# Windowed attention and mixture of experts on one core: a new order of the opening, of the keys, of the sum transposes and of the projection

## The chip, the core and the metric

The kernel runs on one core of a Trainium2 chip. The metric is the time of one execution on the device, in microseconds (us). TensorE (PE) does matmuls and transposes and writes to eight PSUM banks; ScalarE (ACT), VectorE (DVE) and GpSimd (POOL) do the rest, GpSimd without access to PSUM; SyncE (SP) issues most of the DMA transfers. Each engine works through its own instructions in order, and the engines are tied to each other by semaphores alone.

## The reference

Two stages, each added to its input. The first is a windowed attention with a mixed score; the second a mixture of eight experts of which two are taken.

```python
t = _ln_c(x) @ W_prep + b_prep            # 5 x 8 heads x 32: q_n, q, k, k_m, v; windows of 8 x 8 tokens
bias, pat_n, pat_m = _spatial(intrinsic)  # relative tables, gathered by the offset of two tokens
score = bias + einsum('bhod,ohid->bohi', q_n, pat_n) \
      + einsum('bhod,bhid->bohi', q, k) + einsum('bhid,ohid->bohi', k_m, pat_m)
score = (score - mean) / sqrt(var(score, ddof=1) + 1e-5)
x = x + (einsum('bohi,bhid->bohd', score, v)) @ W_fin + b_fin
xt = _ln_t(x)                             # 2048 tokens, 64 channels
top 2 of softmax(xt @ Wr + br) -> weights
x = x + sum over the two of weight * (gelu((layernorm(xt) * ln_g + ln_b) @ W1 + b1) @ W2 + b2)
```

## The kernel before

There are 2048 tokens in 32 windows, handled as 16 pairs (`NPAIR`) in four groups (`NG`) of four pairs.

**PSUM.** `make_plan` lists every use of a bank in the order in which TensorE fills it, as (use, bank, readers); from it `begin` takes how often the bank must have been drained, `filled` and `drained` what its readers and their successors wait for. `pe_steps(t)` gives TensorE's uses in step t of the main loop.

**Opening.** x is loaded in four parts, two by SP's queue and two by ScalarE's. VectorE takes the moments of all 16 pairs (`bn_stats`, `bn_aggr`) and then the inverse roots RS by three rounds of an iteration on all 16 columns (`inverse_root`). The normalised XN of pairs 0 to 7 is made by VectorE, of 8 to 11 by ScalarE, of 12 to 15 by GpSimd. GpSimd first makes the identity IDN, issues six small loads (RB, LNB) and then makes the constants CEN, BPS and SEL. TensorE warms up with eight matmuls (`warm`), folds the weights (`weights`, bank 6; ScalarE copies them to WT_ with two copies), and then makes both tables: `table("tm")` and `table("tn")`. The transposes `xt` turn XN into XF.

**Patterns and the round trip.** `pattern("m", m)` makes two tiles of k_m against its table (TAM), for m from 0 to 7. ScalarE copies the even and VectorE the odd tiles to TMG (`copy_moved`), and SP stores each to DRAM (`moved`, L331). When all sixteen stores have landed (`moved_out`), SP loads the same data in another order to SCN (L336), and `pattern("n", m)` may begin: its tiles TNT lie where TMG lay. Behind the n patterns TensorE has the mixed keys (`mixed_keys`, banks 4 to 7, copied to Y), the centred x (`centred`, copied to XC), the shift of the expert bias (`shift_bias`), then the first values and scores. `products` makes the operand AT of the keys behind m pattern 3. Then each n tile is transposed (`turned`), and VectorE adds it to SCN (L1093); every fourth tile (2, 6, 10, 14) goes through a copy HOP by ScalarE to GpSimd (L418). The adds wait for all loads (`moved_in`), the first SR for all adds.

**Main loop, steps 0 to 15.** Step t gives the score of pair t: scores and values (in twos, in even steps), VectorE's SR (L1146), ScalarE's square SQ and copies BV and OR, TensorE's weighted values `o`. For every group j: squares summed on TensorE (`ss`, step 4j+5), copied by ScalarE to SSB, transposed (`st`, L741), from which VectorE makes the variance VB; GpSimd takes the root RSC by a power (L437); VectorE scales to ON (step 4j+9); TensorE turns ON (`on`), ScalarE copies it to ONT, TensorE projects (`y`, L761), VectorE adds to XR (L1182) and takes moments; then normalisation (Z, Z2), transposes (`x2`), the router's logits (`lg`) and its chain on VectorE, tanh on ScalarE, the gates PG (L1175), which GpSimd widens to PW.

**From step 16 on** TensorE has four hidden products of two matmuls each per step (L702, L703), the products down (L714), the gate transposes `gb` (L786), and what is left of the chain above for the later groups.

In steps 6, 10 and 14 of the kernel before, the first of TensorE's uses is this:

```python
        if t % 4 == 2 and t >= 6:
            s.append((("st", (t - 6) // 4), 5, 1))
```

## Time and profile before

| | us |
|---|---|
| median of 3 runs | 210.13 (207.98 to 211.75) |
| profiled execution, its own time | 211.79 |
| its span, first to last instruction | 210.0 |
| TensorE busy | 179.1 (85%) |
| ScalarE busy | 114.5 (55%) |
| VectorE busy | 107.9 (51%) |
| GpSimd busy | 70.5 (34%) |

Busy shares are means over stretches that differ. The order of time shows each engine's work with the idle time ahead of it and what ended that; the chain of waits follows the last instruction back to what released it. A granted clock of 1.00 is 2.4 GHz on TensorE, 0.50 is 1.2 GHz. Matmuls overlap, so that a mean duration is longer than the distance from one to the next.

### The profile page before, as it was taken

The page shows a single profiled execution, that of the slowest core. Times are in us where ns is not written, and L with a number is a line of the kernel's source. Part 1 is how long each engine was busy: PE and PEld are TensorE (multiplying, and loading weights), DVE is VectorE, ACT ScalarE, POOL GpSimd, SP SyncE. Part 2 cuts the span into 40 slices and gives each one's busy share as a digit, 9 for nine tenths or more (in the row PEclk, how much of TensorE's full clock was granted, in tenths as well). Part 3 has the DMA queues.
Part 4 walks back from the last instruction along what each step waited for, and adds up shares of the span by engine and source line. Part 5 has one row for each costly group of instructions (what it writes and reads, how often), then busy time and mean ns, then how long its engine had stood idle before and what let it go on. Part 6 is the DMA issues. An engine that isn't in the chain of part 4 may idle for free.

```text
span 210.0 us, 4283 instructions
## 1 busy us (share of the span) xinstructions
PE 179.1 (85%) x1590; PEld 113.5 (54%) x1590; DVE 107.9 (51%) x298; ACT 114.5 (55%) x225; POOL 70.5 (34%) x104
## 2 busy tenths in 40 slices
PE   6678980899999696758878959999999999999983
PEld 6486430232499574635746925657466745666531
DVE  3642550256637732333476683157864874574333
ACT  2082770246524559573964755765676475666740
POOL 7568100000004700280945928083650056012000
PEclk9856996589999969995896997999999999999999
DMA  6840597699900000200030000000000000000000
GB/s 166 208 116 0 197 331 276 145 227 224 205 4 2 3 0 3 78 25 3 0 101 3 0 5 0 2 0 3 0 25 0 3 0 25 0 2 3 27 0 25
DMA packets 10356, 12.80 MB, mean 61 GB/s; under 512 B 2072, under 2 KB 7712, under 8 KB 10336
## 3 DMA queue, kind: packets, MB, share of 16 engines
q1 hardware_dynamic: 9712, 12.25, 22.0%
q10 hardware_dynamic: 432, 0.27, 0.5%
q8 instruction: 13, 0.21, 0.4%
q14 instruction: 7, 0.06, 0.1%
q0 software_dynamic: 192, 0.01, 0.1%
HBM read 7.81 MB, written 4.72 MB: 60 GB/s over the span
## 4 chain that ended last, share of the span: by engine, by line
PE 65%; ACT 10%; DVE 6%; POOL 6%; issue 6%; SPq 2%; DMA 2%; DVEq 0%; ACTq 0%; POOLq 0%
PE PS L714 12%; PE PS L553 7%; PE PS L702 6%; PE PS L703 6%; PE PS L615 4%; PE PS L786 4%; PE PS L568 4%; PE PS L578 3%; POOL RSC L437 3%; PE PS L761 3%; SPq L331 2%; ACT BV L912 2%; DMA moved<-TMG 2%; PE PS L585 2%; PE PS L642 2%
## 5 line engine op out<-in xcount | busy, mean ns | idle before, releaser
L935 ACT ACTIVATE HR<-PS,B1P 128x512 f32<-128x512 f32 x64 | 39.0, 693 | 5.0 <-PE PS L703 5.0
L714 PE MATMUL PS<-HR,W2s 128*64 128x512 f32 x128 | 31.0, 605 | 0.0
L702 PE MATMUL PS<-X,W1H 128*128 128x512 f32 x64 | 27.4, 428 | 0.0
L703 PE MATMUL PS<-X,W1L 128*128 128x512 f32 x64 | 26.1, 407 | 0.0
L1005 ACT ACTIVATE GB<-PS 128x512 f32<-128x512 f32 x16 | 9.6, 598 | 23.4 <-PE PS L786 23.4
L437 POOL TENSOR_TENSOR RSC<-VB,NHALF 128x32 f32<-128x32 f32 x4 | 21.8, 5461 | 0.3
L425 POOL COPY PW<-PG 128x512 f32<-128x512 f32 x16 | 10.4, 683 | 32.7 <-DVE PG L1175 32.5
L418 POOL TENSOR_TENSOR SCN<-HOP,SCN 128x512 f32<-128x512 f32 x4 | 6.2, 1553 | 44.5 <-ACT HOP L923 44.5
L1146 DVE TENSOR_TENSOR SR<-PS,SCN 128x512 f32<-128x512 f32 x16 | 10.6, 687 | 17.8 <-PE PS L615 14.5
L912 ACT ACTIVATE BV<-PS 64x256 f32<-64x256 f32 x32 | 12.2, 383 | 13.6 <-PE PS L599 13.0
L862 ACT ACTIVATE TMG<-PS 128x512 f32<-128x512 f32 x16 | 10.1, 648 | 16.0 <-PE PS L553 16.0
L553 PE MATMUL PS<-TAN,XF 64*32 64x512 f32 x128 | 10.9, 816 | 6.9 <-DMA moved<-TMG 6.9
L714 PEld LDWEIGHTS PS<-HR,W2s 128*64 128x64 f32 x128 | 7.8, 136 | 13.6 <-issue 12.7
L702 PEld LDWEIGHTS PS<-X,W1H 128*128 128x128 f32 x64 | 12.5, 195 | 3.1 <-issue 0.8
L681 PE MATMUL PS<-BV,SR 128*64 128x66 f32 x256 | 11.7, 242 | 2.6 <-issue 2.2
L786 PEld LDWEIGHTS PS<-IDN,PW 128*128 128x128 f32 x64 | 6.7, 140 | 13.2 <-issue 12.4
L1128 DVE SCALAR_TENSOR_TENSOR GM<-PS,B,GB 128x512 f32<-128x512 f32 x12 | 9.0, 751 | 9.3 <-ACT GB L1005 7.9
L703 PEld LDWEIGHTS PS<-X,W1L 128*128 128x128 f32 x64 | 12.6, 196 | 2.2
L681 PEld LDWEIGHTS PS<-BV,SR 128*64 128x64 f32 x256 | 9.8, 150 | 5.5 <-issue 5.4
L966 ACT ACTIVATE SQ<-SR 128x512 f32<-128x512 f32 x16 | 10.0, 628 | 3.8 <-DVE SR L1146 3.7
L840 DVE COPY TMG<-PS 128x512 f32<-128x512 f32 x8 | 5.6, 698 | 12.2 <-PE PS L553 12.2
L615 PE MATMUL PS<-Y,XF 64*64 64x256 f32 x128 | 11.2, 478 | 0.4 <-DVE SR L1146 0.4
(144 smaller groups left out, 314.6 us busy)
## 6 DMA issues: line engine op xcount, KB each, us to landing
moved<-TMG SPq DMA_DIRECT2D x16, 256.0 KB, 2.8
SCN<-moved SPq DMA_DIRECT2D x16, 256.0 KB, 7.8
W1R<-in_W SPq DMA_DIRECT2D x4, 256.0 KB, 4.0
W1E<-in_W SPq DMA_DIRECT2D x2, 256.0 KB, 5.4
W2s<-in_W SPq DMA_DIRECT2D x1, 512.0 KB, 3.7
out<-XR SPq DMA_DIRECT2D x4, 128.0 KB, 1.8
REL<-in_rel SPq DMA_DIRECT2D x2, 225.0 KB, 5.2
XR<-in_x SPq DMA_DIRECT2D x2, 128.0 KB, 2.4
```

The lines of the kernel that those rows point to most:

```text
L425: G.tensor_copy(PW[:, ep, :, :, :], PG[j % 2][:, :, 2 * ep:2 * ep + 2].unsqueeze(3) .to_broadcast([P, 4, 2, C])).then_inc(gates_wide, 1)
L437: G.tensor_tensor(RSC[:, :, :, :].rearrange("p q h g -> p (q h g)"), vb, NHALF[:, :], ALU.pow).then_inc(rsc_ready, 1)
L553: last = nc.tensor.matmul(PS[before[(kind, 2 * m + r)][0]][32 * u:32 * u + 32, :], XF[rows, :, token], window, start=True, stop=True)
L615: m = nc.tensor.matmul(dst, XF[rows, 2 * (t + a) + b, :], Y[rows, 4 * g:4 * g + 4, t // 2, C * b:C * b + C], start=True, stop=True)
L681: m = nc.tensor.matmul(dst, SR[t % 3][:, (2 * h + b) * C:(2 * h + b) * C + C], BV[t % 4][:, b, h, :, :].rearrange("p g d -> p (g d)"), sta ...
L702: nc.tensor.matmul(ps[:, :], W1H[:, col:col + P], X2[:, j * 512:j * 512 + 512], start=True, stop=False)
L703: end(nc.tensor.matmul(ps[:, :], W1L[:, col:col + P], X2[:, j * 512:j * 512 + 512], start=False, stop=True), "h", n)
L714: m = nc.tensor.matmul(ps[d * C:d * C + C, :], W2s[:, 2 * (2 * ep + d) + c, :], HR[(4 * u + 2 * c + d) % 8][:, :], start=(c == 0), stop=(c ...
L786: m = nc.tensor.transpose(ps[:, q * P:q * P + P], PW[:, a % 4, q, :, :].rearrange("p d c -> p (d c)"), IDN[:, :])
L912: last = A(BV[tv % 4][g * C:g * C + C, :, :, g, 0:HD].rearrange("p b h d -> p (b h) d"), PS[b][g * C:g * C + C, 0:256].rearrange("p (n d) ...
L935: A(HR[n % 8][:, :], PS[b][:, :], ACT.Gelu, bias=B1P[:, col:col + 1]).then_inc(bank_drained[b], 1)
L1146: V_.tensor_tensor(SR[t % 3][:, :].rearrange("p (h b o) -> p h b o", h=4, b=2), PS[t % 2][:, :].rearrange("p (h b o) -> p h b o", h=4, b=2 ...
```

## The change

**Opening.** `inverse_root` is gone. VectorE aggregates each part of x right after its statistics. GpSimd takes the roots by a power with NHALF, first for pairs 0 to 11, then for 12 to 15, and makes RS and NB. VectorE makes XN of pairs 0 to 7, 14 and 15, ScalarE of 8 to 13. The six loads of RB and LNB are issued by ScalarE. `warm` takes a count: 8, then 7 between the bias matmul of `weights` and its other matmuls, and 3 behind it. ScalarE copies the m part of the folded weights first (`wt_ready`), the rest behind its XF copies. Only `table("tm")` stands ahead of the transposes `xt`, which run in the order 0, 2, 1, 3 on banks 4, 7, 5, 0; the copies of tables and XF are divided anew. `table("tn")` stands behind m pattern 1, `products` behind m pattern 4 (their copies behind tiles 2 and 8 on ScalarE).

**Keys.** Mixed keys, centred x and the bias shift stand ahead of the n patterns on TensorE, and their copies ahead of the stores of turned tiles on ScalarE and VectorE. TensorE's own wait for `moved_out` ahead of n is gone; the copies of n keep theirs.

**Adds.** GpSimd's four tiles are 1, 4, 7 and 10 (`HOPS`).

**Steps.** `st` stands at the end of steps 6, 10 and 14, behind `on` and ahead of `x2`; `x2` of group 0 moves from bank 5 to bank 4. On VectorE the addition of the projection and its moments stand ahead of the gates.

```diff
-    plan += [(("tn", h), (4, 5, 7, 6)[h], 1) for h in range(4)]
-    plan += [(("xt", j), j, 1) for j in range(NG)]
+    plan += [(("xt", j), (4, 5, 7, 0)[j], 1) for j in (0, 2, 1, 3)]
...
-        if t % 4 == 2 and t >= 6:
-            s.append((("st", (t - 6) // 4), 5, 1))
...
-        return s + late(10, (("on", 0), 4), (("on", 1), 7)) + late(14, (("x2",), 5)) \
-            + late(11, (("y",), 4)) + late(15, (("lg",), 5))
+        return s + late(10, (("on", 0), 4), (("on", 1), 7)) + late(6, (("st",), 5)) \
+            + late(14, (("x2",), 4)) + late(11, (("y",), 4)) + late(15, (("lg",), 5))
...
+            step(pool.memset(NHALF[:, :], -0.5))
...
-            pool.wait_ge(rx_ready, 1)
-            for q in range(12, NPAIR):
-                last = G.tensor_scalar(XN[:, q, :, :], twice(XR[:, q, :]), RS[:, q:q + 1], NB[:, q:q + 1],
-                                       ALU.mult, ALU.add)
-            last.then_inc(xn3_ready, 1)
+            for part, cols in enumerate((slice(0, 12), slice(12, NPAIR))):
+                pool.wait_ge(mvx_ready, part + 1)
+                step(G.tensor_scalar(VE[:, cols], MV[:, cols, 1], 0.0, EPS_C, ALU.max, ALU.add))
+                step(G.tensor_scalar(RA[:, cols], MV[:, cols, 0], -1.0, None, ALU.mult))
+                G.tensor_tensor(RS[:, cols], VE[:, cols], NHALF[:, cols], ALU.pow).then_inc(rs_ready, 1)
+                pool.wait_ge(rs_ready, part + 1)
+                G.tensor_tensor(NB[:, cols], RA[:, cols], RS[:, cols], ALU.mult).then_inc(rx_ready, 1)
...
             for m in range(8):
                 pattern("m", m)
-                if m == 3:
+                if m == 1:
+                    pe.wait_ge(*drained("wt"))
+                    pe.wait_ge(reln_in, 16)
+                    pe.wait_ge(rel0_in, 16 * 4)
+                    pe.wait_ge(sel_ready, 1)
+                    table("tn")
+                if m == 4:
                     products()
             for h in range(4):
                 pe.wait_ge(*drained("a", h))
             for h in range(4):
                 pe.wait_ge(*drained("tn", h))
-            pe.wait_ge(moved_out, 16 * 16)
-            for m in range(8):
-                pattern("n", m)
             for m in range(8):
                 mixed_keys(m)
             for j in range(NG):
...
             shift_bias()
+            for m in range(8):
+                pattern("n", m)
...
-            for d in range(2):
-                last = A(WT_[:, :, :, d, :], PS[6][:, :].rearrange("p (k g c) -> p k g c", k=4, g=2), ACT.Copy)
-            last.then_inc(bank_drained[6], 1)
...
+            weight_copies(KM, KM + 1).then_inc(wt_ready, 1)
+            for part, qs in enumerate(((8, 9, 10, 11), (12, 13))):
+                act.wait_ge(rx_ready, part + 1)
+                for q in qs:
+                    last = A(XN[:, q, :, :], twice(XR[:, q, :]), ACT.Identity, scale=RS[:, q:q + 1], bias=NB[:, q:q + 1])
                 last.then_inc(xn2_ready, 1)
...
             for j in range(NG):
                 dve.wait_ge(x_in[j], 16)
                 for q in range(4 * j, 4 * j + 4):
                     last = V_.bn_stats(BNX[:, q, :], XR[:, q, :])
-            step(last)
-            for q in range(NPAIR):
-                last = V_.bn_aggr(MV[:, q, :], BNX[:, q, :])
...
-            inverse_root(RS[:, :], VE[:, :], RA[:, :])
...
+                step(last)
                 for q in range(4 * j, 4 * j + 4):
+                    last = V_.bn_aggr(MV[:, q, :], BNX[:, q, :])
+                if j >= 2:
+                    last.then_inc(mvx_ready, 1)
+            for part, qs in enumerate(((0, 1, 2, 3), (4, 5, 6, 7), (14, 15))):
+                dve.wait_ge(rs_ready, 1 if part < 2 else 2)
...
+            dve.wait_ge(moved_out, 16 * 16)
+            for tile in range(1, 16, 2):
+                store_turn(dve, V_.tensor_copy, tile)
             dve.wait_ge(moved_in, N_MOVED)
             for tile in range(16):
-                if tile % 4 == 2:
+                if tile in HOPS:
```

In VectorE's steps the block of `t - 16` (PG) moves, unchanged, from ahead of the block of `t - 12` (XR and `moments`) to behind it. The loop on GpSimd over four hops takes `tile = HOPS[k]`, with `HOPS = (1, 4, 7, 10)`.

## Rows read from the trace of the kernel before

**Rows 1.** The chain of waits: start us, us, what; stores and turned tiles.

```profile
33.40 3.81 DMA moved<-TMG
...
63.65 7.26 PE PS L578 x64
```

**Rows 2.** The order of time, opening: start us, us, engine, line, operation, count, [idle before].

```profile
1.24 0.93 ACTq L857 DMA_DIRECT2D XR<-in_x  x2
...
1.59 3.78 PE L509 MATMUL PS<-IDN 128*128 128x128 f32 x16 [1.59 <-POOL IDN L364]
...
1.77 2.37 POOL L367 DMA_DIRECT2D RB<-in_rel  x4 [0.23 <-issue]
...
4.76 0.60 DVE L1047 BATCH_NORM_STATS2 BNX<-XR 128x6 f32<-128x64 f32 x4 [0.28 <-DMA XR<-in_x]
...
7.89 2.41 PE L502 MATMUL PS<-CEN,WS 64*128 64x64 f32 x16
...
10.34 1.08 ACT L866 ACTIVATE WT__81<-PS 128x512 f32<-128x512 f32 x2 [6.64 <-PE PS L502]
...
11.31 1.64 ACT L871 ACTIVATE XN<-XR,NB,RS 128x128 f32<-128x128 f32 x4
...
16.38 3.49 PE L642 MATMUL PS<-IDN,XN 128*128 128x128 f32 x16
...
20.87 4.31 PE L553 MATMUL PS<-TAM,XF 64*32 64x512 f32 x64 [0.99 <-ACT XF L879]
```

**Rows 3.** Busy time by stretch: us, engines (instructions), granted clock, DMA share, GB/s.

```profile
9.30:19.50 10.20, 8.93 (x69) 8.22 (x68) 4.48 (x18) 5.07 (x11) 6.60 (x14) 0.50 0.25 65
...
37.50:43.40 5.90, 5.85 (x56) 2.13 (x64) 1.70 (x3) 1.55 (x3) 0.00 (x0) 0.50 0.81 184
...
125.20:208.00 82.80, 79.83 (x411) 47.25 (x408) 46.58 (x126) 49.69 (x87) 26.14 (x39) 0.98 0.02 6
```

**Rows 4.** The order of time: stores, loads, and the n patterns.

```profile
22.75 11.10 SPq L331 DMA_DIRECT2D moved<-TMG  x16
...
37.22 11.38 SPq L336 DMA_DIRECT2D SCN<-moved  x16
...
37.55 10.95 PE L553 MATMUL PS<-TAN,XF 64*32 64x512 f32 x128 [6.90 <-DMA moved<-TMG]
```

**Rows 5.** The line of the loads: issues, and time to landing.

```profile
L336 SPq DMA_DIRECT2D SCN<-moved x16: 616/617/1057, 37.2 to 47.5; - x16
...
DMA to landing us min/median/max: 3.8/7.8/11.8
```

**Rows 6.** The order of time: the adds of turned tiles, and the first SR.

```profile
64.34 7.31 DVE L1093 TENSOR_TENSOR SCN<-PS,SCN 128x512 f32<-128x512 f32 x12 [1.94 <-PE PS L578]
...
72.94 1.29 DVE L1146 TENSOR_TENSOR SR<-PS,SCN 128x512 f32<-128x512 f32 x2 [1.28 <-POOL SCN L418]
```

**Rows 7.** TensorE's groups to 125 us: line, form, count | busy, mean ns | idle before.

```profile
L691 PE MATMUL PS<-SQ,ONES 128*32 128x512 f32 x32 | 4.3, 604 | 2.4 <-DVE XR L1182 2.4
L761 PE MATMUL PS<-WF,ONT 128*128 128x64 f32 x32 | 4.0, 277 | 0.7 <-ACT ONT L952 0.7
...
L741 PE MATMUL PS<-IDN,SSB 128*128 128x128 f32 x12 | 2.4, 335 | 7.2 <-ACT SSB L979 7.2
```

**Rows 8.** GpSimd's groups, whole span: the powers of 32 and 4 columns.

```profile
L437 POOL TENSOR_TENSOR RSC<-VB,NHALF 128x32 f32<-128x32 f32 x4 | 21.8, 5461 | 0.3
...
L453 POOL TENSOR_TENSOR RZ<-RZ,NHALF 128x4 f32<-128x4 f32 x4 | 4.2, 1042 | 0.3
```

**Rows 9.** ScalarE's groups from 72 to 125 us.

```profile
L912 ACT ACTIVATE BV<-PS 64x256 f32<-64x256 f32 x27 | 10.3, 383 | 10.2 <-PE PS L599 9.7 <-PE PS L681 0.2
...
L988 ACT ACTIVATE W1H<-W1R,LNG 128x256 fp32r<-128x256 f32 x8 | 3.6, 514 | 0.0
```

**Rows 10.** The order of time: a power on GpSimd beside VectorE's products.

```profile
108.96 1.04 POOL L453 TENSOR_TENSOR RZ<-RZ,NHALF 128x4 f32<-128x4 f32 x1
109.05 1.42 DVE L1166 TENSOR_TENSOR ON<-OR,RSC 128x256 f32<-128x256 f32 x4
```

More of the change, by code:

```diff
@@ L504, in weights, with warm @@
                 end(m, "wt")
-            def warm():
-                for _ in range(8):
+            def warm(times):
+                for _ in range(times):
                     nc.tensor.matmul(PS[7][:, 0:P], IDN[:, :], IDN[:, :], start=True, stop=True)
@@ L644, in _ @@
                 end(m, "xt", j)
+            for h in range(4):
+                pe.wait_ge(*drained("tm", h))
             for j in range(NG):
@@ L664, in _ @@
             shift_bias()
+            for m in range(8):
+                pattern("n", m)
             pe.wait_ge(wv_in, 32)
@@ L893, in _ @@
             A(WRR[:, 0, :], WRs[:, :], ACT.Copy).then_inc(wrh_ready, 1)
-            act.wait_ge(moved_out, 16 * 16)
-            for tile in range(0, 16, 2):
-                store_turn(act, act_copy, tile)
             for m in range(8):
@@ L901, in _ @@
                 A(XC[:, 512 * j:512 * j + 512], PS[j][:, :], ACT.Copy).then_inc(bank_drained[j], 1)
+            act.wait_ge(moved_out, 16 * 16)
+            for tile in range(0, 16, 2):
+                store_turn(act, act_copy, tile)
             def value_copies(tv):
@@ L1020, in _ @@
             V_ = nc.vector
-            def inverse_root(y, v, work):
-                step(V_.tensor_scalar(y.bitcast(I32), v.bitcast(I32), -0.5, float(0x5F3759DF), ALU.mult, ALU.add))
-                for _ in range(3):
-                    step(V_.scalar_tensor_tensor(out=work, in0=y, scalar=-0.5, in1=y, op0=ALU.mult, op1=ALU.mult))
-                    step(V_.tensor_tensor(work, work, v, ALU.mult))
-                    step(V_.scalar_tensor_tensor(out=y, in0=work, scalar=1.5, in1=y, op0=ALU.add, op1=ALU.mult))
             def moments(xin, j):
```

110 lines of the change are left out of this document (52 added, 58 removed).

## The prediction

> **What bounds the kernel now.** I read the chain of waits first, then the order of time engine by engine, then the busy table of chosen stretches, then the groups by line. Four stretches stand out.
>
> The opening ends at 20.87 us, when the first m pattern starts [rows 2]. Ahead of it come, one behind the other, the folded weights, both tables and sixteen transposes, nearly all at a granted clock of 0.50, the lower level of 1.2 GHz [rows 2, 3].
>
> Then comes a round trip through DRAM. The m patterns go out as sixteen stores from 22.75 us on; the last has landed at 33.40 + 3.81 = 37.2 us [rows 1, 4], and only then may TensorE start the n patterns, because TNT is TMG: it sits idle for 6.90 us [rows 4] and comes back at clock 0.50, so that the first n patterns run at half rate [rows 3]. The loads of the same data back are issued from 37.22 us on; the last was issued at 47.5 us and took the longest to land, 11.8 us, so all are in at 59.3 us [rows 5]. VectorE starts to add the turned n tiles to them at 64.34 us [rows 6]. So the loads are 5.0 us early there, and TensorE's queue sets the time: n, keys, centring, bias shift, first values and scores.
>
> Third, steps 0 to 16 of the main loop, from the first SR at 72.94 us [rows 6] to about 125 us. TensorE waits 7.2 us in all for the copies SSB ahead of the sum transposes, which stand at the head of steps 6, 10 and 14, and 2.4 us for XR ahead of the last squares [rows 7].
>
> Last, from 125.2 us on, TensorE is busy for 79.83 of 82.80 us at clock 0.98 [rows 3]: bound by its own work, which the change leaves as it is. An earlier start there passes straight to the end.
>
> **The opening.** GpSimd loses six DMA issues, of which four took 2.37 us [rows 2]. They go to ScalarE's queue, where two issues take 0.93 us: six are 2.8 us, from 2.2 to 5.0 us, then the table load and the dummy Gelu. ScalarE's next work, the weight copy, starts at 10.34 us today [rows 2]; that cover hides them, without it they would cost their 2.8 us. With CEN and BPS some 3.4 us earlier, the bias matmuls follow the eight warm-ups, which end at 5.4 us [rows 2], and seven more warm-ups fill the time until the weights come; I leave the weight matmuls' start at 7.9 us, as today. They took 2.41 us [rows 2], the last of them at the lower clock [rows 3]. With TensorE busy ahead of them I take 1.8 us, end 9.7; the bound above is 10.3.
>
> The roots: sixteen columns of moments are gathered with VectorE's statistics, the third group of which runs at 4.76 us [rows 2]; its own aggregation follows now, so that GpSimd has twelve columns at about 6.1 us. It needs two small operations (0.6 us) and a power. No row shows 12 columns; 32 take 5461 ns and 4 take 1042 ns [rows 8]: the bounds are 5.5 and 1.0 us, and a straight line between them gives 2.3, which I take, since both rows are this operation. The roots are there at 9.1 us; today ScalarE's XN starts at 11.31 [rows 2]. The other four columns follow at 11.2 us.
>
> From there ScalarE is the longest: the weight copy for KM alone (a quarter of the columns of a pair that took 1.08 us [rows 2]; 0.6 us by estimate) to 10.3, six XN at 1.64 / 4 = 0.41 us [rows 2] to 12.8, then two tables and two XF at 0.54, half of that pair, to 14.9. VectorE (ten XN, two tables, two XF) ends about then too. TensorE needs the m table and the transposes ahead of m. Both tables lie between 11.4 and 16.38 us today, the m table being a third of their instructions: 1.7 us, and the transposes take 3.49 us [rows 2]; at the upper clock half of each, 2.6 us, hides under the copies. At the lower clock m starts at 17.1. I take 15.1 us for the first m pattern, a gain of 5.8; the bounds are 14.7 and 17.1.
>
> **The round trip and the fill.** Today the stores are done 16.3 us after the first m pattern (20.87 to 37.2). The n table now sits behind the second m pair (two thirds of 5.0 us, at the upper clock 1.6), while its TAN copies, for which TensorE pauses today, run beside the third and fourth pair: these nearly cancel. The other weight copies (0.9 us on ScalarE) fall before its first m tile is complete. I take 16.0: stores done at 31.1 us. SyncE's queue is otherwise unchanged, so the loads take their 59.3 - 37.2 = 22.1 us again and are in at 53.2 us.
>
> TensorE's m stage takes 37.55 - 6.90 - 20.87 = 9.8 us today [rows 2, 4]; with the n table 11.3, so it is free at 26.4 us. Keys to first scores take 63.65 - 48.50 = 15.1 us (first turned tile less the end of the n patterns [rows 1, 4]), and most of it now stands where the idle time is. The eight n pairs took 10.95 us [rows 4]; without the idle ahead they run like the m patterns, 64 instructions or four pairs in 4.31 us [rows 2]: 8.7. The first turned tile is there at 26.4 + 15.1 + 8.7 + 0.5 = 50.7 us, so now the loads are the later ones, by 2.5 us: VectorE starts at 53.2 instead of 64.34 us. 5.0 of this is the fill, 6.1 the earlier stores. Keys queued ahead of n delay n only where it would have waited; behind ScalarE's and VectorE's waits for the stores no key copy is queued any more. The bias shift takes its wait for LNB along, whose loads now start before 5 us.
>
> **The adds.** Twelve take 7.31 us, and the first SR waits a further 1.28 us for GpSimd's last add [rows 6]. With GpSimd's four at tiles 1, 4, 7 and 10 its last ends before VectorE's. Gain 1.2 us; bounds 0, because VectorE's last four tiles now follow each other, and 1.3. The first SR stands at 60.6 instead of 72.94 us: 12.3 us.
>
> **Sum transposes at a step's end.** I laid out steps 5 to 16, each instruction after its predecessor on its engine and after what it waits for. The scores of step 6 no longer stand behind the first SSB: they start 2.0 us earlier, the first root 1.8. In step 10 TensorE no longer waits for an SSB that itself stands behind the ON products: the second root starts 4.8 us earlier. New waits appear. The projection of step 11 waits for ONT behind ScalarE's value copies (383 ns each), squares and W1H [rows 9]: 3.1 us, where 0.7 is seen today [rows 7]. In step 14 x2, on bank 4 now, waits for ONT's first half, and y waits for X2's low half (0.9 us). The third root comes 5.0 us early, the second group of hidden matmuls 4.8. So of 9.6 us of waits about half is given back. I take 4.5; bounds 0 (all of it returns at ONT) and 7.
>
> What queues behind the later wait for the transposed sums on VectorE is the odd SR; the layout has it 0.2 us late at step 6. Projection ahead of gates: XR and its moments go ahead of PG, which waits for tanh at that point anyway; gb, for which PG is needed, comes two groups of matmuls later, so I cost it at nothing. Uncovered it would cost 1.4 us three times.
>
> **Sum.** 5.0 (fill) + 6.1 (opening) + 1.2 (adds) + 4.5 (steps) = 16.8 us. The profiled execution took 211.79 us, its span 210.0; less 16.8 that is 195.0. The median of the runs is 1.66 below it: 193.3, say 193.5.
>
> **A row against a rule.** While GpSimd's power ran for 1.04 us from 108.96 us on, VectorE's four ON products, two SBUF inputs each, took 1.42 us from 109.05 us on [rows 10]: neither waited for the other. The Trainium skill, "SBUF — State Buffer", section "Who interferes with whom", says that a VectorE instruction with two SBUF inputs and a GpSimd instruction that reads SBUF exclude each other for a whole instruction. The trace does not agree; by the rule rival 3 would hold.
>
> **The rivals.**
> 1. The steps give all back: ONT and the roots become the waits. For it: 2.4 us more at step 11 already; against it: the second root no longer waits behind the scores. 193.5 + 4.5 = 198.
> 2. The clock stays at 0.50 through tables, transposes and the first m pairs. For it: so it was from 9.3 to 19.5 us with TensorE busy for 8.93 of 10.2 us [rows 3]; against it: the added warm-ups. First m at 17.1 and up to 2 us more until the stores are done: 195.5 to 197.5.
> 3. GpSimd's second root chain (1.04 us and three small operations) holds up XN on VectorE, then its tables and XF: +1.6, 195. [rows 10] speak against it.
> 4. The loads flow faster and TensorE sets the adds at 50.7 us: 191.
> 5. Slower than before: the clock stays at 0.50 from the first m pattern to the first turned tile. At the upper clock that stretch is 36 us long; at the lower I estimate 26 us more, since copies hide some. The first SR comes at 86.5 us, 13.5 later than today, less 4.5: 219. It decides from 16.8 us of loss on. The longest such stretch here is 10.2 us, and idle time preceded it [rows 3].
> 6. The opening gives nothing (the power at its upper bound, the weights late): 193.5 + 6.1 = 199.5.
>
> **How the numbers follow.** Forecast 0.50, with a range of its own of 191.5 to 195.5; rivals 1 to 6: 0.18, 0.15, 0.04, 0.07, 0.02, 0.04. The range reaches from below rival 4 to above rival 6, 189.5 to 200.5, with both bounds of the steps in it. A difference of 2%, 4.2 us, is about what a measurement here can tell from no change. Only rival 5 is slower; two rivals at once come near 204. Faster 0.95, same 0.03, slower 0.02.
>
> **What would show it.** Right: first m pattern near 15 us; no TensorE gap at the stores; VectorE's first add waiting for a load; SR not waiting for GpSimd; no idle time ahead of the sum transposes, and ONT the new wait. Wrong: clock 0.50 between 12 and 22 us; a first add at 56 us or later; the second group of hidden matmuls less than 3 us nearer to the first SR.

## The result and the profile after

Four runs of the changed kernel have a median of 201.06 us (200.42 to 201.88), four of the kernel before 210.54 us (207.98 to 211.75). The ratio is 0.959 with a 95% interval of 0.949 to 0.969: faster, by about half of what was forecast (193.5 us), and 0.56 us above the end of the range. The profiled execution took 201.88 us, its span is 200.1 us. The same kernel ran four more times in a later group, on another chip: 198.78 us (197.73 to 200.50), ratio 0.949 (0.939 to 0.959). Single executions that lie more than 1.5% above the fastest of their kernel are left out of ratios, and where fewer than three are left of a kernel below, or of the kernel before beside it, the median stands without a ratio.

The spans are best compared mark by mark. "Again" is the profile of that later group, same code; "held" is the profile of run d2 below, the changed kernel with three edits of mine.

| us | before | forecast | after | again | held |
|---|---|---|---|---|---|
| first m pattern | 20.87 | 15.1 | 15.85 | 15.54 | 14.83 |
| first m pattern to last store landed | 16.33 | 16.0 | 19.13 | 17.26 | 16.83 |
| last store to last load landed | 22.17 | 22.1 | 22.30 | 22.10 | 21.81 |
| last load to VectorE's first add | 4.97 | 0 | 0.03 | 0.02 | 0.02 |
| first add to first SR | 8.60 | 7.4 | 10.72 | 9.61 | 7.94 |
| first SR to second hidden group | 52.23 | 47.7 | 48.29 | 48.34 | 47.70 |
| second hidden group to the end | 84.9 | 84.9 | 83.8 | 83.8 | 83.7 |
| span | 210.0 | 193.2 | 200.1 | 196.7 | 192.8 |

Each row is the difference of two starts or landings in the trace; the forecast is the prediction's own sum, laid out on the same marks. After against forecast, the 6.9 us lost are 0.75 + 3.13 + 0.2 in the opening and the round trip, 3.3 in the adds and 0.6 in the steps, less 1.1 us won in the last stretch.

The order of time of the changed kernel, to be laid beside [rows 2], [rows 4] and [rows 6] (start us, us, engine, line, operation, count, [idle before]):

```profile
5.13 0.60 DVE L1050 BATCH_NORM_STATS2 BNX<-XR 128x6 f32<-128x64 f32 x4 [1.09 <-DMA XR<-in_x]
...
7.83 2.30 POOL L385 TENSOR_TENSOR RS<-VE,NHALF 128x12 f32<-128x12 f32 x1
...
8.01 2.00 PE L499 MATMUL PS<-CEN,WS 64*128 64x64 f32 x16
...
10.17 2.84 DVE L1059 SCALAR_TENSOR_TENSOR XN<-XR,MV,RS 128x128 f32<-128x128 f32 x10 [2.21 <-POOL RS L385]
...
11.29 1.04 POOL L385 TENSOR_TENSOR RS<-VE,NHALF 128x4 f32<-128x4 f32 x1
...
15.85 3.77 PE L550 MATMUL PS<-TAM,XF 64*32 64x512 f32 x32 [1.12 <-ACT XF L889]
...
21.37 1.95 ACT L868 ACTIVATE TAN<-PS 128x450 f32<-128x450 f32 x4 [1.16 <-PE PS L523]
...
42.51 8.79 PE L550 MATMUL PS<-TAN,XF 64*32 64x512 f32 x128
...
52.88 1.97 PE L575 MATMUL PS<-IDN,TMG 128*128 128x128 f32 x16
...
57.31 1.89 DVE L1093 TENSOR_TENSOR SCN<-PS,SCN 128x512 f32<-128x512 f32 x3 [5.18 <-DMA SCN<-moved]
...
58.15 8.21 PE L575 MATMUL PS<-IDN,TMG 128*128 128x128 f32 x48 [3.30 <-DVE SCN L1093]
...
62.69 0.69 DVE L1093 TENSOR_TENSOR SCN<-PS,SCN 128x512 f32<-128x512 f32 x1 [1.01 <-PE PS L575]
...
68.03 1.29 DVE L1148 TENSOR_TENSOR SR<-PS,SCN 128x512 f32<-128x512 f32 x2 [0.30 <-DVE SCN L1093]
...
104.23 0.63 PE L780 MATMUL PS<-IDN,Z 128*128 128x128 f32 x4 [3.55 <-ACT ONT L963]
...
106.36 3.64 PE L762 MATMUL PS<-WF,ONT 128*128 128x64 f32 x16 [0.43 <-DVE X L1206]
...
116.32 0.50 PE L703 MATMUL PS<-X,W1H 128*128 128x512 f32 x1
```

What to see. The reorder of the keys does what the prediction said: the n patterns at 42.51 us follow the keys without idle time and take 8.79 us (8.7 forecast), and VectorE now waits 5.18 us for a load. But TensorE may not run on: four turned tiles fill its four banks, and behind them it stands idle for 3.30 us until VectorE's first add frees one. The next twelve tiles (48 instructions) take 8.21 us, and it is now VectorE that waits for TensorE between its adds (`62.69`, 1.01 us). In step 14 there is a second new wait, x2 for ONT, 3.55 us, and behind it the projection takes 3.64 us for 16 matmuls; the second hidden group starts at 116.32 us.

The busy table shows why both are slow. Columns: stretch, its length, PE, PEld, DVE, ACT and POOL busy (instructions), granted clock, DMA share, GB/s.

```profile
15.80:19.60 3.80, 3.75 (x36) 1.44 (x36) 0.69 (x1) 1.12 (x2) 3.30 (x10) 0.55 0.08 27
...
42.50:51.30 8.80, 8.66 (x134) 3.23 (x135) 5.22 (x9) 4.46 (x7) 0.00 (x0) 1.00 1.14 226
...
58.10:66.40 8.30, 8.25 (x52) 8.12 (x56) 5.61 (x9) 1.79 (x3) 5.30 (x4) 0.65 0.01 2
104.80:115.10 10.30, 9.87 (x61) 8.72 (x60) 6.02 (x19) 4.42 (x9) 4.72 (x1) 0.50 0.01 2
116.30:199.90 83.60, 78.36 (x412) 46.38 (x408) 47.78 (x127) 49.49 (x87) 26.69 (x40) 1.00 0.02 7
```

The n patterns ran at 1.00 (0.50 in the first part of the stretch before [rows 3]); the first m pairs, the turned tiles behind the wait and step 14 ran wholly or mostly at 0.50, the lower level of 1.2 GHz. The last stretch had 1.00 instead of 0.98, which is the 1.1 us that nobody forecast: 0.50 had stood at its head before, from 125.36 us on.

The chain of waits holds the round trip (start us, us, what), beside [rows 1]:

```profile
21.37 1.95 ACT TAN L868 x4
23.33 0.50 ACT TMG L868
...
31.46 3.53 DMA moved<-TMG
...
46.20 11.09 DMA SCN<-moved
```

The stores now hang on the four TAN copies: m tile 4's copy stands behind them on ScalarE. The last store has landed at 31.46 + 3.53 = 34.99 us, the last load at 57.29.

### The profile page after: what moved, and what is told of

It reads as the page before. It is cut to its first block, busy times and chain, and to the rows that moved or that the text cites. A ratio compares the mean times of both kernels' runs of the same rounds, so it can differ in the third digit from the quotient of the medians.

```text
span 200.1 us, 4320 instructions
## 1 busy us (share of the span) xinstructions
PE 176.6 (88%) x1610; PEld 114.1 (57%) x1610; DVE 109.2 (55%) x290; ACT 114.9 (57%) x227; POOL 69.7 (35%) x102
## 4 chain that ended last, share of the span: by engine, by line
PE 48%; POOL 15%; DMA 9%; issue 7%; SPq 7%; ACT 6%; DVE 5%; DVEq 0%; ACTq 0%; POOLq 0%
PE PS L715 12%; POOL RSC L433 8%; PE PS L703 6%; PE PS L704 6%; DMA SCN<-moved 6%; SPq L337 5%; PE PS L575 4%; PE PS L787 4%; PE PS L550 4%; PE PS L762 3%; DMA XR<-in_x 2%; PE PS L682 2%; DMA moved<-TMG 2%; POOL RS L385 2%; SPq L332 1%
## 5 line engine op out<-in xcount | busy, mean ns | idle before, releaser
L421 POOL COPY PW<-PG 128x512 f32<-128x512 f32 x16 | 10.1, 664 | 39.1 <-DVE PG L1186 38.9
L433 POOL TENSOR_TENSOR RSC<-VB,NHALF 128x32 f32<-128x32 f32 x4 | 21.8, 5458 | 0.3
L575 PE MATMUL PS<-IDN,TMG 128*128 128x128 f32 x64 | 10.2, 335 | 3.3 <-DVE SCN L1093 3.3
L1093 DVE TENSOR_TENSOR SCN<-PS,SCN 128x512 f32<-128x512 f32 x12 | 7.7, 686 | 7.9 <-DMA SCN<-moved 5.2
L575 PEld LDWEIGHTS PS<-IDN,TMG 128*128 128x128 f32 x64 | 9.7, 179 | 3.9 <-issue 3.9
```

What stands on the lines that cost most here:

```text
L421: G.tensor_copy(PW[:, ep, :, :, :], PG[j % 2][:, :, 2 * ep:2 * ep + 2].unsqueeze(3) .to_broadcast([P, 4, 2, C])).then_inc(gates_wide, 1)
L433: G.tensor_tensor(RSC[:, :, :, :].rearrange("p q h g -> p (q h g)"), vb, NHALF[:, :], ALU.pow).then_inc(rsc_ready, 1)
L575: m = nc.tensor.transpose(ps[:, h * P:h * P + P], TNT[:, tile, h * P:h * P + P], IDN[:, :])
```

## The experiments

Four groups, each on another chip; in each the kernel before ran beside the others. The first two (a, b) undo or fill one thing each, the third (c) joins what helped, the last (d) tests the best. The changed kernel itself ran beside them only in the third (c0), so a, b and d are held against its two medians, 201.06 and 198.78 us, from other chips. These differ by more than 2 us themselves, so that a median of one edit tells little here; the marks within the profiles carry the argument. The ratios of the third and fourth group rest on three and four executions of the kernel before. A fill is a number of matmuls of IDN by IDN into a free bank whose result nobody reads; `warm` gets the bank as an argument.

### a1: fill behind the fourth turned tile

```diff
                 turned(tile)
+                if tile == 3:
+                    pe.wait_ge(*drained("v", 1))
+                    warm(15)
```

> Only difference to the changed kernel: behind the fourth turned tile TensorE waits for the copies of value 1 and then runs 15 warm-up matmuls (about 3.2 us at the upper clock) into the free bank 7, where it now stands idle for 3.3 us waiting for the loads. Theory 1 (the wait for the loads puts the clock down, and the turned tiles that follow run at half rate, so that TensorE paces the adds): granted clock near 1.00 from 57 to 64 us, adds from first add to first SR 7.5 to 8.6 us instead of 10.7, time 198 to 199. Rival (the adds are long because the last four tiles now all fall to VectorE): clock or not, adds stay near 10.7 us and the time at 201.

Measured: 200.69 us in median (197.91 to 201.50), the profiled execution 201.50. First add at 55.38, first SR at 64.21: 8.83 us at a clock of 1.00 throughout. The fill was too long. TensorE's and VectorE's order of time:

```profile
52.52 1.95 PE L506 MATMUL PS<-IDN 128*128 128x128 f32 x16
55.47 1.83 PE L506 MATMUL PS<-IDN 128*128 128x128 f32 x14 [0.99 <-issue]
57.13 5.40 PE L575 MATMUL PS<-IDN,TMG 128*128 128x128 f32 x48
...
115.95 0.50 PE L706 MATMUL PS<-X,W1H 128*128 128x512 f32 x1
```

```profile
58.20 5.70 DVE L1096 TENSOR_TENSOR SCN<-PS,SCN 128x512 f32<-128x512 f32 x9 [0.94 <-PE PS L575]
```

The fill ends at 57.3 us, 1.9 us behind the first add (0.99 us of this is the stop within it), and VectorE waits 0.94 us for it. Without that wait the adds would take 7.9 us. The twelve tiles behind it take 5.40 instead of 8.21 us. The profile then has 0.50 from 84.84 to 95.08 us, which the profile after has not, and from 105.32 to 115.56 us, as the profile after has. From the first SR to the second hidden group it takes 51.74 us instead of 48.29, with the same instructions in these steps, so the gain does not reach the end, and the 198 to 199 us of theory 1 did not come. What follows: with the wait filled the twelve tiles ran at 1.00, and a gain there can be lost to another stretch at 0.50.

### a2: fill in the opening

```diff
                 if j == 3:
                     pe.wait_ge(xn_ready, 3)
+                    pe.wait_ge(*drained("tm", 2))
+                    warm(2, 2)
...
+            pe.wait_ge(*drained("tm", 3))
+            warm(5, 3)
             for h in range(4):
                 pe.wait_ge(*drained("tm", h))
```

> Only difference to the changed kernel: 2 warm-up matmuls ahead of the last transposes of the opening and 5 ahead of the first m pattern, into banks 2 and 3 once their tables are copied, where TensorE stands idle for 0.8 and 1.1 us. Theory 1 (those idle times put the clock at 0.50 from 16.1 to 19.5 us): the first two m pairs take about 2 us together instead of 3.8, the n table follows 1.8 us earlier, the stores are done at about 33.3 us instead of 35.0, time 199 to 199.5. Rival (the stores are paced by the transfers themselves and by the copies of the n table ahead of tile 4): the m pairs are faster but the stores are done at 34.5 us or later, time 200.5 to 201.

Measured: 198.58 us (198.13 to 201.93), where 199 to 199.5 were expected. The first two m pairs took 2.1 us instead of 3.77, the stores had landed 17.29 us after the first m pattern. But in every other profile of this study the first m pairs ran at 1.00 too, with the opening unchanged; only the profile after shows 0.50 there. What follows: half clock in the first m pairs is worth about 1.7 us where it occurs, and this run can't say that the fill prevents it.

### a3: the hops back at 2, 6, 10, 14

```diff
-HOPS = (1, 4, 7, 10)
+HOPS = (2, 6, 10, 14)
```

> Only difference to the changed kernel: GpSimd's four tiles are 2, 6, 10 and 14 again. Theory 1 (TensorE at half rate paces the adds): adds from first add to first SR stay at 10.3 to 11.3 us, time 200.5 to 201.5. Rival (the new division of the tiles makes them long): 8.6 us as in the kernel before, time about 199.

Measured: 200.88 us (200.28 to 202.79). From the first add to the first SR it is 10.86 us, as theory 1 said, not 8.6. VectorE's order of time has the old wait for GpSimd again:

```profile
62.85 2.48 DVE L1093 TENSOR_TENSOR SCN<-PS,SCN 128x512 f32<-128x512 f32 x4 [0.18 <-PE PS L575]
66.61 1.29 DVE L1148 TENSOR_TENSOR SR<-PS,SCN 128x512 f32<-128x512 f32 x2 [1.28 <-POOL SCN L414]
```

The wait is 1.28 us against 0.30 in the profile after, but the twelve adds ahead of it take 9.59 us (55.74 to 65.33) against 10.42. Both profiles have 6.8 us at 0.50 there. So the edit of the hops is worth 0.98 us in the wait and only 0.14 us in the distance (10.72 against 10.86) while TensorE sets the pace. In the median it doesn't show (200.88 against 201.06 and 198.78 us).

### a4: keys, centring and bias shift behind the n patterns again

```diff
-            for m in range(8):
-                mixed_keys(m)
-            ...
-            shift_bias()
-            for m in range(8):
-                pattern("n", m)
+            pe.wait_ge(moved_out, 16 * 16)
+            for m in range(8):
+                pattern("n", m)
+            for m in range(8):
+                mixed_keys(m)
+            ...
+            shift_bias()
```

with the plan of the banks and both engines' copies in the old order. 

> Only difference to the changed kernel: keys, centred x and bias shift stand behind the n patterns again, with TensorE's wait for the stores ahead of n. By the step of the prediction (the fill is worth 5.0 us): 205 to 206. Theory 1 (most of the fill turns into a wait for the loads, and that wait costs the clock): first add at 61 to 62 us, set by TensorE again, adds 7.5 to 8.6 us, first SR at 69.5 to 70.5 instead of 68.0, time 202 to 203.

Measured: 203.69 us (203.33 to 203.83). TensorE, then VectorE, in the order of time:

```profile
32.57 10.09 PE L550 MATMUL PS<-TAN,XF 64*32 64x512 f32 x128 [6.31 <-DMA moved<-TMG]
```

```profile
58.50 7.82 DVE L1094 TENSOR_TENSOR SCN<-PS,SCN 128x512 f32<-128x512 f32 x12 [1.94 <-PE PS L575]
66.62 1.29 DVE L1149 TENSOR_TENSOR SR<-PS,SCN 128x512 f32<-128x512 f32 x2 [0.30 <-DVE SCN L1094]
```

The idle time ahead of n is back, and the first add comes 58.50 - 54.01 = 4.5 us after the last load. But TensorE now has no wait between the turned tiles, the clock there is 1.00, and from the first add to the first SR it is 8.12 us, not 10.72 or 9.61. So the fill is worth 4.5 us at the first add, as forecast (5.0), and only 1.9 to 3.0 at the first SR. The first add and the first SR came 3 us earlier than theory 1 named them, since the stores had landed earlier too (32.2 us against 35.0); the 8.12 us are as named. In the medians the whole edit is worth 2.6 us (203.69 against 201.06) to 4.9 us (against 198.78), and the time lies below the 205 to 206 us by the prediction's step. It holds a loss elsewhere besides: the profile has 0.50 from 87.08 to 97.32 us and takes 51.67 us from the first SR to the second hidden group instead of 48.29.

### b1: ONT ahead of the square

```diff
+                    output_transposed(t)
                     act.wait_ge(*drained("score", t))
                     A(SQ[:, t, :]
...
-                if t < LAG:
-                    output_transposed(t)
```

> Only difference to the changed kernel: ScalarE copies ONT ahead of the square of the same step instead of behind it. Theory: x2 waits for ONT's first half only because ScalarE does that copy behind the square of SR 14, which stands behind Z2 on VectorE; done ahead, x2 waits for Z2 alone: wait in step 14 about 1.4 us instead of 3.55, projection of step 11 no later, second hidden group 46 us after the first SR instead of 48.3, time 198.5 to 200. Rival (the wait moves to Z2, GpSimd's roots and the logits chain): 200.5 to 201.

Measured: 198.10 us (196.23 to 199.59), ratio 0.947 (0.937 to 0.957). TensorE in step 14:

```profile
100.61 0.66 PE L780 MATMUL PS<-IDN,Z 128*128 128x128 f32 x4 [1.64 <-DVE Z L1196]
...
103.46 3.65 PE L762 MATMUL PS<-WF,ONT 128*128 128x64 f32 x16 [1.56 <-DVE X L1205]
```

The wait for ONT is gone, but x2 then waits 1.64 us for Z, and the projection 1.56 us for X2's low half: 3.2 of 4.0 us are only renamed, and the clock falls here as in the kernel without the edit. From the first SR to the second hidden group it is 47.46 us against 48.29 (46 expected).

### b2: two of the four TAN copies on VectorE

```diff
                 if tile == 2:
-                    for h in range(4):
+                    for h in range(2):
                         copy_table(act, act_copy, "tn", h)
...
                 copy_moved(dve, V_.tensor_copy, tile)
+                if tile == 3:
+                    for h in range(2, 4):
+                        copy_table(dve, V_.tensor_copy, "tn", h)
```

> Only difference to the changed kernel: two of the four copies of the n table go to VectorE. If these copies ahead of tile 4 on ScalarE hold up the stores (which stand still for 2.8 us after the fourth), the second half of the stores starts 0.7 to 0.9 us earlier and the loads are in 0.7 to 0.9 us earlier after the first m pattern (41.4 us in the changed kernel's profile; 39.4 to 40.0 where the first pairs ran at the upper clock), time 200 to 200.4. Rival (the transfers pace them): no difference, 201.

Measured: 198.22 us (198.19 to 204.77), ratio 0.951 (0.943 to 0.958). The stores have landed 16.81 us after the first m pattern, against 17.26 to 17.51 us in the eight profiles that have four copies on ScalarE and the first m pairs at 1.00 (a1 to a4, b1, b3, b4 and the changed kernel again); the five later profiles with the edit (c1 to c3, d1, d2) lie at 16.75 to 16.90. That is 0.4 to 0.8 us less, where 0.7 to 0.9 were expected and none by the rival. ScalarE's TAN copies take 1.04 us instead of 1.95.

This profile holds a second answer, by chance. Its turned tiles and adds are the changed kernel's, the wait as well, but the clock stayed at 1.00 until 64.00 us. TensorE, then VectorE:

```profile
54.95 5.43 PE L575 MATMUL PS<-IDN,TMG 128*128 128x128 f32 x48 [3.05 <-DVE SCN L1096]
```

```profile
54.11 7.64 DVE L1096 TENSOR_TENSOR SCN<-PS,SCN 128x512 f32<-128x512 f32 x12 [4.88 <-DMA SCN<-moved]
62.05 1.29 DVE L1151 TENSOR_TENSOR SR<-PS,SCN 128x512 f32<-128x512 f32 x2 [0.30 <-DVE SCN L1096]
```

Three profiles, the same instructions in this stretch, a wait of 3.0 to 3.3 us. Twelve tiles took 5.43, 7.10 and 8.21 us (b2, again, after), and first add to first SR 7.94, 9.61 and 10.72 us. The differences are the same to the hundredth: 1.67 and 2.78 us. Six more profiles with the changed kernel's hops and this wait unfilled (a2, b1, b3, b4, c1, c2) lie in between, the adds each time 2.5 us longer than the twelve tiles. So what differs in the adds is TensorE's clock there, and nothing else. Of the ten profiles with the wait unfilled (2.7 to 3.7 us; these nine and a3) all but b2 fell to 0.50 there.

### b3: RB and LNB issued after x has landed

```diff
-            for h in range(4):
-                act.dma_start(RB ...
             act.wait_ge(x_in[0], 16)
             A(WARM[:, :], XR[:, 0, 0:1], ACT.Gelu)
+            act.wait_ge(x_in[3], 16)
+            for h in range(4):
+                act.dma_start(RB ...
```

> Only difference to the changed kernel: ScalarE issues the six loads of RB and LNB only once all of x has landed. Theory: these loads delayed the second part of x (landed at 5.11 us instead of 3.85), and with it the roots by 1 us. Expected: second part of x back at 3.9 us, first power on GpSimd at 6.9 instead of 7.83, first m pattern 0.6 to 0.9 us earlier, time 200.3. Rival: the part lands late anyway, no difference.

Measured: 201.79 us (200.29 to 203.61), ratio 0.968 (0.954 to 0.981). VectorE's statistics of the second part of x still start late:

```profile
4.85 0.60 DVE L1051 BATCH_NORM_STATS2 BNX<-XR 128x6 f32<-128x64 f32 x4 [0.88 <-DMA XR<-in_x]
```

With RB issued early the same start lies at 5.13 us in the profile after and at 5.14 in b1, and that part of x has landed at 3.96 us in a3 and at 3.98 in a2. It differs from execution to execution with this part of the code unchanged. The theory that the six loads on ScalarE's queue hold up x is not borne out: the part came late without them and early with them.

### b4: fill ahead of x2 in step 14

```diff
+                        if a == 0:
+                            pe.wait_ge(*drained("v", NPAIR - 2))
+                            warm(15, 6)
                         pe.wait_ge(z2_ready, a + 1)
                         ps = begin("x2", a)
```

> Only difference to the changed kernel: in step 14 TensorE runs 15 warm-up matmuls (about 3.2 us at the upper clock) into bank 6, free there, ahead of the x2 transposes, where it stands idle for 3.55 us. Theory 1 (that new wait costs its clock afterwards: the projection y took 3.64 us instead of 1.97, the hidden matmuls of step 16 3.6 instead of 1.9): no stretch at 0.50 from 104 to 116 us, second hidden group about 44 to 45 us after the first SR instead of 48.3, time 197 to 198. Rival (the clock does not matter there, the chain over VectorE and GpSimd sets the pace): distance stays at 48 us, time 201.

Measured: 197.98 us (197.67 to 198.37), ratio 0.950 (0.943 to 0.956). TensorE:

```profile
98.48 3.51 PE L506 MATMUL PS<-IDN 128*128 128x128 f32 x30
102.20 0.63 PE L783 MATMUL PS<-IDN,Z 128*128 128x128 f32 x4 [0.20 <-ACT ONT L966]
...
104.33 1.97 PE L762 MATMUL PS<-WF,ONT 128*128 128x64 f32 x16 [0.89 <-DVE X L1209]
...
112.25 0.50 PE L703 MATMUL PS<-X,W1H 128*128 128x512 f32 x1
```

x2 comes no earlier for it, since ONT sets it. The projection takes 1.97 us instead of 3.64, and from x2 to the second hidden group it is 10.05 instead of 12.09 us. The clock's share of the step's new wait is 2.0 us. But the distance of theory 1 did not come: from the first SR to the second hidden group it is 47.67 us (44 to 45 expected, 48.29 without the fill). This profile has 0.50 from 65.73 to 69.14 us, just behind its first SR, where the profile after has 1.00, and x2 starts 37.62 us behind the first SR instead of 36.20. So 1.4 of the 2.0 us were lost ahead of x2, and 0.6 reached the second hidden group. A stretch at 0.50 from 106.69 to 110.11 us is left too. The medians of b1, b2 and b4 (198.0 to 198.2 us) are not told apart from the 198.78 us of the changed kernel run again (c0).

### c0 to c3: the changed kernel again, and combinations

c0 is the changed kernel. c1 is b2 and b4 together; c2 is b2, b1 and eight matmuls ahead of x2 instead of fifteen; c3 is c1 with nine matmuls behind the fourth turned tile.

> The changed kernel, unchanged, as the base of this group. By the theory that the clock makes the spread: within 200 to 202 us in median, the turned tiles at a clock of 0.50 for at least 3 us, adds (first add to first SR) 9.3 to 10.9 us, a wait of about 3.5 us ahead of x2 in step 14 followed by several us at 0.50. The first m pairs at either clock, so that first m to the last store landed is 17.3 to 17.5 us or 19.1 us.

> Two of the four TAN copies go to VectorE, and 15 matmuls that nobody reads stand ahead of x2 in step 14. If the opening's distance and the lower clock behind the wait for ONT are two separate losses, their gains add up: alone they gave 198.2 and 198.0 us against 201 us, so about 195.5 us is expected, with 16.8 us from the first m pattern to the last store landed and y at full clock (about 2.0 us). If both only shift where the clock falls (a later stretch falls instead), 198 us, as each alone.

> As the run with the TAN copies divided, and ScalarE's copies ONT ahead of the square in steps 11 and 14, with 8 matmuls that nobody reads ahead of x2, since the wait there is then 1.6 us. By the theory that the wait is to be shortened rather than filled: 0.3 to 1.0 us under the run with 15 matmuls ahead of x2, 194.5 to 195.5 us. By the rival that X2's low half sets y anyway (1.56 us seen when ONT went first): no lower than that run, and a fall of the clock at y where the short fill does not reach.

> As the run with the TAN copies divided and the 15 matmuls ahead of x2, and 9 more that nobody reads behind the fourth turned tile, where TensorE waits for the first add. If the adds are longer because of the lower clock behind that wait: adds 7.4 to 8.0 us at a clock of 1.00, first SR at 61.5 to 62 us, 0.5 to 2 us under the run without them. If the loads still set the adds' start and VectorE's own 7.3 us their length: no difference, with the clock at 1.00.

Measured: c0 198.78 us (197.73 to 200.50). c1 201.18 us (197.26 to 203.08): neither the 195.5 us of the sum nor the 198 of the rival came, and its executions lie too far apart to decide; the profiled one had 0.50 behind the fourth turned tile and again from 86.49 to 96.73 us. c2 198.74 us (196.08 to 199.44), ratio 0.944 (0.930 to 0.958), where 194.5 to 195.5 were expected; its profile has 0.50 from 86.25 to 96.49 us as well. c3 196.20 us (195.04 to 201.47), ratio 0.936 (0.924 to 0.948). The adds of c0, TensorE then VectorE:

```profile
55.76 7.10 PE L575 MATMUL PS<-IDN,TMG 128*128 128x128 f32 x48 [3.02 <-DVE SCN L1093]
```

```profile
59.10 0.69 DVE L1093 TENSOR_TENSOR SCN<-PS,SCN 128x512 f32<-128x512 f32 x1 [0.95 <-PE PS L575]
```

c0's expectation was half wrong: its median is 1.2 us below the 200 us named, though its adds (9.61 us) and its wait in step 14 (3.56 us, then 0.50 from 101.41 to 111.65 us) are as named. c3 gave the adds the 7.4 to 8.0 us expected (7.64 + 0.30 = 7.94) with the first SR at 61.63 us. Whether shortening the wait in step 14 is worth more than filling it, c2 does not tell, since c1 gives no median to hold it against.

### d1 and d2: c3 with step 10 filled, and c3 again

```diff
+                        if a == 0:
+                            pe.wait_ge(*drained("st", 0))
+                            warm(5 + half, 5)
                         pe.wait_ge(on_ready, 4 * a + 2 * half + 2)
```

> The fastest kernel so far (TAN copies divided, matmuls that nobody reads behind the fourth turned tile and ahead of x2), and 5 and 6 more such matmuls in step 10, ahead of the two halves of on, where TensorE stands idle for 1.35 and 1.62 us and where two profiles of this study fell to a clock of 0.50 for 10 us. If these waits make the clock fall there: no 0.50 between 83 and 97 us, all executions at 195 to 196 us, and an execution like the fourth of the run without this (201.5 us) does not occur. If the fall there has another cause: one or more executions at 199 to 202 us again, with the same idle time filled.

> The fastest kernel so far again, unchanged, beside the one with step 10 filled: by the theory that step 10's waits make the clock fall there in some executions, most executions at 195 to 196.5 us and some at 199 to 202 us; by the rival, the same spread as its neighbour.

Measured, six executions each: d1 195.65 us (194.28 to 196.32), ratio 0.936 (0.929 to 0.942); d2 195.09 us (194.67 to 195.42), ratio 0.934 (0.930 to 0.939). This is the fastest version found, 3.7 us below the changed kernel's better median and 6.0 below the other; its six executions lie below all eight of the changed kernel (197.73 to 201.88). TensorE and VectorE of d2 at the adds, to be laid beside the rows after:

```profile
49.80 1.97 PE L575 MATMUL PS<-IDN,TMG 128*128 128x128 f32 x16
51.61 2.17 PE L506 MATMUL PS<-IDN 128*128 128x128 f32 x18
54.33 5.43 PE L575 MATMUL PS<-IDN,TMG 128*128 128x128 f32 x48 [0.55 <-DVE SCN L1102]
```

```profile
53.49 7.64 DVE L1102 TENSOR_TENSOR SCN<-PS,SCN 128x512 f32<-128x512 f32 x12 [4.43 <-DMA SCN<-moved]
61.43 1.29 DVE L1157 TENSOR_TENSOR SR<-PS,SCN 128x512 f32<-128x512 f32 x2 [0.30 <-DVE SCN L1102]
```

And the page's row of the granted clock, in tenths, 40 slices of the span; first the profile after, then d2:

```profile
PEclk9996999999966999999995599999999999999999
```

```profile
PEclk9999999999999699999997999999999999999999
```

VectorE's adds follow each other without a gap, and in the four profiles with this wait filled (a1, c3, d1, d2) the tiles ran at 1.00. 0.50 is left in d2 for 3.4 us twice, one of them behind the 1.86 us for which TensorE waits ahead of the first weighted values. d1 and d2 are the same within their spread, and none of d2's six executions lay above 195.42 us, so the rival came: the two idle times of step 10 cost nothing that filling them brings back. Why some profiles (a1, a4, c1, c2) show 0.50 for 10.2 us from 85 to 87 us on, and why one execution of c3, the same kernel as d2, took 201.47 us, stays open.

## Why the prediction was wrong in size

The direction held, and so did most of the layout; the sum promised 16.8 us and 9.9 came, in the later group 13.4 (spans). Two of its terms were mis-sized. The adds, put at a gain of 1.2 us, were a loss of 2.1 (after) and 1.0 (again); the opening with the earlier stores, put at 6.1, gave 2.2 and 4.4. One of the prediction's own signs of being wrong, a first add at 56 us or later, showed in the profile after (57.31) and not in the later one (54.92).

**The step that failed: the adds, behind the fill.** The prediction said "now the loads are the later ones, by 2.5 us: VectorE starts at 53.2", and took 7.4 us from there to the first SR, as if TensorE would then simply be ahead. It did not ask what TensorE does while it is early. It can be ahead by four banks only, so the fill that removes the 6.90 us of idle time ahead of n [rows 4] puts 3.3 us of idle time behind the fourth turned tile. The clock may fall in or just behind it. Then the tiles no longer feed the adds fast enough: 10.72 us (after) or 9.61 us (again) in place of 7.4. The same instructions at 1.00 took 7.94 us (b2), and with the wait filled 7.94 us too (d2). So 2.8 of the 3.3 us are the clock, and 0.5 us is the term's own error: against the kernel before the wait behind the adds shrank from 1.28 to 0.30 us, but the twelve adds took 7.64 us instead of 7.31 [rows 6], so the hops gave 0.7 us of the 1.2 at 1.00, and 0.14 us with TensorE setting the pace (a3).

**The fill itself.** 5.0 us forecast, 4.97 gone at the first add, 4.5 lost when it is undone (a4). Right in size; what it gave at the first SR was less by what the new wait cost.

**The opening.** The first m pattern came at 15.85 us (15.1 forecast; 14.79 to 15.91 in all profiles). The straight line for the power of 12 columns gave 2.3 us, measured 2.30. The weights were 0.2 us slower than taken, and started at 8.01 us. The roots were ready at 10.1 us instead of 9.1, because VectorE's statistics of the second part started at 5.13 us, where the prediction had taken 4.76 for the third.

**The round trip.** "These nearly cancel" was wrong: the 16.0 us kept from the first m pattern to the last store were 17.3 us in profiles at 1.00, since the four TAN copies (1.95 us) stand ahead of m tile 4 on ScalarE, and the stores behind them; with the copies divided they were 16.8 (b2, d2), so these copies explain 0.5 us and the other 0.8 stays open. In the profile after they were 19.13, and 1.66 us of that is the first two m pairs at 0.50 (3.77 against 2.11 us). The prediction hid a ScalarE term under TensorE's. The loads' 22.1 us were right (21.8 to 22.3).

**The steps.** 4.5 us forecast, 3.94 measured (after) and 3.89 (again). Right in size, though partly by luck: both kernels have several us at 0.50 in this stretch, and with the same instructions in the steps it was 48.24 to 51.74 us in other profiles (a1 to a4, b2, b3). In a1 and a4 a further 10.2 us at 0.50 left 0.5 us of the gain. TensorE's wait ahead of the sum transposes is gone, as forecast. The new wait stands elsewhere: not in step 11 (0.32 us where 3.1 were forecast) but in step 14, where x2 waits 3.55 us for ONT, and it cost 2.0 us more through the clock behind it (b4, where 0.6 us of them reached the second hidden group). The prediction had that wait without a price.

**The rivals.** Rival 1 (all given back by the steps) fell by those 3.9 us; what came near it in a1 and a4 was the clock. Rival 4 (TensorE sets the adds) fell by VectorE's wait for the loads in all profiles but a4, rival 5 by the time. Rival 6 (the opening gives nothing) named 199.5 us, between the two medians, but not for its reason: the first m pattern came 5.0 us earlier. Rival 2 (0.50 through tables, transposes and the first m pairs) came half true in one profile: tables and transposes ran at 1.00, the first m pairs at 0.50. Rival 3 fell by the trace: VectorE's ten XN took 2.84 us, 0.284 each, beside GpSimd's power of 1.04 us, which took what it takes alone [rows 8]. The Trainium skill, "SBUF — State Buffer", section "Who interferes with whom", would have the two exclude each other; for this power the trace does not agree.

The prediction's row against that rule speaks for the small power alone, though. VectorE's ON products of the third group, beside GpSimd's copy PW of 128x512, in the profile after and then in d2:

```profile
116.37 1.84 DVE L1168 TENSOR_TENSOR ON<-OR,RSC 128x256 f32<-128x256 f32 x4
116.60 0.67 POOL L421 COPY PW<-PG 128x512 f32<-128x512 f32 x1 [7.08 <-DVE PG L1186]
```

```profile
109.03 1.43 DVE L1177 TENSOR_TENSOR ON<-OR,RSC 128x256 f32<-128x256 f32 x4
109.26 1.67 POOL L421 COPY PW<-PG 128x512 f32<-128x512 f32 x1 [4.90 <-DVE PG L1195]
```

Each time one of the two is held up: the products take 1.84 us instead of the 1.43 of the other groups, or the copy 1.67 us instead of the 0.61 it takes alone. Why the power differs was not tried. The 0.4 us on VectorE cost nothing in the profile after: it waits 0.60 us for GpSimd's RZ behind them, and TensorE turns these ON only at 122.56 us.

**What would have given the time.** With the TAN copies divided and the two new waits filled, the span is 192.8 us against the forecast's 193.2, and no mark up to the second hidden group lies more than 0.9 us from its place in the forecast; the last stretch, 1.2 us shorter than taken, makes up for it. So the forecast was near that of a kernel whose clock holds at its new waits, partly by luck: two stretches at 0.50 are left in the steps of this profile. That it does not hold was in the profile before: a lower clock behind idle time stands in [rows 3], and rivals 2 and 5 were built on it, but neither at a wait that the change itself makes.

## What to carry to other kernels

A wait of TensorE cost its length here and then, in most profiles, a stretch at half the clock behind it: when an edit fills one idle time, ask where TensorE will be stopped next (banks, not only data), and price both. Where that wait can't be shortened, a few matmuls that nobody reads, ended just before the data come, can give back the clock's share (2.0 us here behind x2, 1.7 to 2.8 us at the adds). Too many of them cost part of it again, and what is won at one place can be lost to a fall of the clock at another, so the gain is read at a mark far behind. When a distance is carried over from the profile before, check each engine in it for work that the change puts in the middle, here ScalarE's four copies ahead of a store.

## What was unexpected in the hardware

- The same instructions fall to the lower clock in one execution and not in another: behind a wait of 3.0 to 3.3 us the profile after had 0.50 for 6.8 us, c0 for 3.4 us, b2 not at all until 64.00 us. Mean granted clocks of the changed kernel's eight executions lie between 0.940 and 0.965, their times between 197.73 and 201.88 us; d2's clocks are 0.980 and above.
- A fill of 30 instructions ran through in 3.51 us ahead of x2 (b4), but behind the fourth turned tile (a1) it stopped for 0.99 us after 16 of them, with no releaser in the trace. Why was not tried.
- GpSimd's copy of 128x512 and VectorE's products of two inputs hold each other up, in 13 profiles of the changed kernel and its variants the products (1.84 us instead of 1.43), in c2 and d2 the copy (1.67 us instead of 0.61). A power of 4 columns and the same products do not (1.04 and 1.42 us [rows 10]).
- TensorE's clock rose while it ran nothing but transposes: the profile after has 0.50 from 58.20 to 63.80 us and 1.00 from 63.90 to 66.30, and turned tiles alone from 58.15 us to there.
- The second part of x landed anywhere from 3.89 us (c3) to 5.12 us (b1), whether or not other loads were issued beside it (b3).
